# Tile 1's attention weights ahead of the turning of the edge records and of tile 0's counts, in a graph network on one core

## The reference

```python
# block 0: attention over the incoming edges of each node
a = hs @ Ws.T + h[dst] @ Wd.T + emb_rel[etype] @ Wr.T      # hs = h[src]
e = leaky_relu((a @ attn_fc2_w.T)[:, 0], 0.01)
w = exp(e - segment_max(e, dst)[dst])
alpha = w / segment_sum(w, dst)[dst]
agg = segment_sum(alpha[:, None] * hs, dst)                # h itself where a node has no edge
x = layernorm(x + agg + h @ loop_weight)
# block 1: two layers of the same form
agg = segment_sum((rel_embed[rel_id] + h[src]) @ W_r, dst)
h = rrelu(agg * deg ** -0.5 + (h @ W_el if no edge else h @ W_sl))
x = layernorm(x + h)
```

## Time and profile before

| | us |
|---|---|
| median of 3 runs | 2778.87 (2776.01 to 2779.62) |
| the profiled execution | 2776.1 |
| its span | 2774.0 |
| tile loop, about | 105 to 2167 |
| PE busy | 2149.1 (77%) |
| DVE busy | 2045.1 (74%) |
| POOL busy | 1591.4 (57%) |
| ACT busy | 1223.8 (44%) |

### The profile page before, as it was taken

How to read it: one execution, slowest core, us unless ns; L and a number is a source line. 1 busy time by engine, 2 the same in 40 slices (tenths; PEclk the granted TensorE clock), 3 DMA queues, 4 the chain that set the end, 5 groups by cost and what they waited for, 6 DMA issues and landing times.

```text
span 2774.0 us, 45483 instructions
## 1 busy us (share of the span) xinstructions
PE 2149.1 (77%) x16208; PEld 1802.6 (65%) x16208; DVE 2045.1 (74%) x4582; ACT 1223.8 (44%) x3215; POOL 1591.4 (57%) x1672
## 2 busy tenths in 40 slices
PE   1366676667767777777787788788787999999998
PEld 0255565556666666666676676676675876888887
DVE  5889998887888888888888888888797456333333
ACT  1255665555556456555555555555555323000000
POOL 6767777777777777777777777777774000000000
PEclk9988887888888988888889888999899999999999
DMA  8545554554555554554555555555454354666664
GB/s 219 145 126 173 173 153 153 157 165 152 160 175 151 156 181 146 159 183 148 160 186 151 160 190 153 168 183 156 148 177 152 112 156 133 215 211 211 217 211 158
DMA packets 184632, 463.50 MB, mean 167 GB/s; under 512 B 86336, under 2 KB 113784, under 8 KB 164577
## 3 DMA queue, kind: packets, MB, share of 16 engines
q1 hardware_dynamic: 116050, 339.10, 36.4%
q0 software_dynamic: 53600, 114.17, 16.4%
q10 hardware_dynamic: 14752, 7.26, 1.0%
HBM read 362.54 MB, written 97.84 MB: 166 GB/s over the span
## 4 chain that ended last, share of the span: by engine, by line
POOL 50%; PE 25%; issue 17%; DVE 6%; DMA 1%; ACT 1%; SPq 1%; ACTq 0%; POOLq 0%; DVEq 0%
POOL arena L559 50%; PE pair L951 19%; DVE arena L1114 2%; PE bank L875 1%; PE pair L924 1%; PE bank L836 1%; PE pair L954 1%; DMA wlp<-n_L_gnn_loop_weight_dram 1%; DVE arena L1084 1%; PE pair L805 1%; PE pair L782 0%; DMA group_starts<-endv 0%; SPq L434 0%; DVE arena L1194 0%; DVE arena L1092 0%
## 5 line engine op out<-in xcount | busy, mean ns | idle before, releaser
L559 POOL DMA_INDIRECT arena<-rows,srcw x1617 | 1541.6, 953 | 518.8 <-issue 491.4
L1114 DVE TENSOR_TENSOR arena<-bank,idx 128x2000 bf16<-128x2000 bf16 (+3 forms) x700 | 560.4, 853 | 21.1 <-PE pair L805 17.9
L951 PE MATMUL pair<-arena 125*125 125x384 bf16 x3285 | 551.4, 326 | 1.6 <-DVE arena L1316 1.6
L805 PE MATMUL pair<-arena 128*128 128x250 bf16 x2500 | 348.9, 287 | 260.0 <-DVE arena L1114 206.5
L581 ACT ACTIVATE arena<-pair 99x264 f32<-99x264 f32 (+2 forms) x410 | 279.0, 712 | 593.8 <-PE pair L805 448.5
L951 PEld LDWEIGHTS pair<-arena 125*125 125x125 bf16 x3285 | 447.4, 136 | 103.3 <-issue 8.4
L675 ACT ACTIVATE arena<-arena,wexp 128x128 f32<-128x128 bf16 x1650 | 487.4, 387 | 1.6
L875 PE MATMUL bank<-arena 128*125 128x130 f32 x3300 | 485.2, 318 | 0.0
L875 PEld LDWEIGHTS bank<-arena 128*125 128x125 f32 x3300 | 474.6, 230 | 4.2
L805 PEld LDWEIGHTS pair<-arena 128*128 128x128 bf16 x2500 | 239.7, 102 | 339.4 <-DVE arena L1114 267.0
L1084 DVE TENSOR_TENSOR arena<-arena,bank 128x4224 bf16<-128x4224 int16 x150 | 344.2, 2350 | 1.7
(11 more groups left out here) (250 smaller groups left out, 2312.6 us busy)
## 6 DMA issues: line engine op xcount, KB each, us to landing
arena<-counts SPq DMA_DIRECT2D x106, 812.5 KB, 4.4
counts<-arena SPq DMA_DIRECT2D x50, 1562.5 KB
arena<-dst SPq DMA_DIRECT2D x50, 1056.0 KB
arena<-etype SPq DMA_DIRECT2D x50, 1056.0 KB
arena<-rows,srcw POOLq DMA_INDIRECT x1617
arena<-counts SPq DMA_DIRECT2D x14, 281.2 KB, 2.8
edge_terms<-arena SPq DMA_DIRECT2D x200, 12.4 KB
xt<-in_x_dram SPq DMA_DIRECT2D x50, 62.5 KB
```

Source lines behind the costliest of these rows:

```text
L559: pool.indirect_dma_start(out=rows[:, q, c, :], out_offset=None, in_=rows0, in_offset=bass.IndirectOffsetOnAxis(ap=srcw[:, q, c:c + 1], ax ...
L805: r = pe.matmul(group_of(n, gi), ohl[:, sl, gi * GC + c, :], ohm[:, sl, gi * GC + c, :], start=(c == 0), stop=(c == GC - 1))
L951: r = pe.matmul(o, ring[0:TN, m % RD, h - h0, :], hs[k][0:TN, h, :], start=(h == first), stop=(h == last - 1))
L1114: return v.tensor_tensor(hot_.rearrange("p c (j t) -> p c j t", t=2), iotap[:, 0:w].rearrange("p (j t) -> p j t", t=2)[:, None, :, :].broa ...
```

## The change

The copies, turns and evacuations of the edge records and the seven count batches of tile 0 leave the first turn and stand in the second: on DVE after `weights(1)` and `prepare_wide(2)`, on PE and ACT after `terms(2)`. `normalise(0)`, `x1_in(0)`, `x1_node(0)`, `node_t(0)` and `node_a(0, 0)`, which stood behind them, so follow at once. PE's `row(0)` comes after the batches of tile 0. `SEQ` is renumbered to fit. POOL's and SP's code is not touched.

```diff
@@ SEQ
     if t_ == 0:
         SEQ["types", 1] = len(SEQ)
         SEQ["turned", 1] = len(SEQ)
+        continue
+    if t_ == 1:
         for b_ in range(NGB):
             SEQ["idx", b_] = len(SEQ)
+        for j_ in range(BT):
+            SEQ["cnt", 0, j_] = len(SEQ)
@@ ACT
                     types_in(1)
                     types(1)
-                    for b in range(NGB):
-                        n = seq("idx", b)
-                        act_evac(act, n, idx[...], slot(n)[...])
-                    for j in range(BT):
-                        batch(0, j)
                     node_t(0)
                     node_a(0, 0)
                 elif t < NT - 1:
+                    if t == 1:
+                        for b in range(NGB):
+                            n = seq("idx", b)
+                            act_evac(act, n, idx[...], slot(n)[...])
+                        for j in range(BT):
+                            batch(0, j)
@@ PE
-                if 1 <= t < NT - 1:
-                    row(t - 1)
-                if t == 0:
-                    types_in(1)
-                    types(1)
+                if t == 1:
                     for b in range(NGB):
...
                     for j in range(BT):
                         batch(0, j)
+                if 1 <= t < NT - 1:
+                    row(t - 1)
+                if t == 0:
+                    types_in(1)
+                    types(1)
                     x1_in(0)
                     x1_node(0)
@@ DVE
                 if t == 0:
                     finalize(0)
                     prepare_edges(1)
+                    normalise(0)
+                if t == 1:
                     for b in range(NGB):
...
                     for j in range(BT):
                         batch(0, j)
-                    normalise(0)
-                elif more:
+                if t >= 1 and more:
                     for j in range(2):
                         batch(t, j)
```

More of the change, by code:

```diff
@@ L686, in act_fast @@
                     types(1)
-                    for b in range(NGB):
-                        n = seq("idx", b)
-                        act_evac(act, n, idx[:, b * GB:(b + 1) * GB, :], slot(n)[:, :].rearrange("p (m g) -> p g m", g=GB))
-                    for j in range(BT):
-                        batch(0, j)
                     node_t(0)
@@ L694, in act_fast @@
                 elif t < NT - 1:
+                    if t == 1:
+                        for b in range(NGB):
+                            n = seq("idx", b)
+                            act_evac(act, n, idx[:, b * GB:(b + 1) * GB, :], slot(n)[:, :].rearrange("p (m g) -> p g m", g=GB))
+                        for j in range(BT):
+                            batch(0, j)
                     for j in range(3):
@@ L1302, in dve_fast @@
                         batch(t, j)
-                else:
+                if not more:
                     finalize(t)
```

## The result

| | before | after |
|---|---|---|
| median (7 runs each) | 2777.42 us (2776.01 to 2779.62) | 2785.93 us (2785.13 to 2790.54) |
| ratio, 95% interval | | 1.0032 (1.0023 to 1.0041) |
| the profiled execution | 2776.1 us | 2787.2 us |
| its span | 2774.0 us | 2785.0 us |

The kernel became 8.5 us slower, by the medians. The forecast was 2787.6, with a range of 2781 to 2793, and 8.7 us for the change itself. Of the 1.7 us between the forecast and the measured 2785.9, 1.5 are the starting value: the forecast stood on a median before of 2778.87 from three runs, and seven runs give 2777.42.

The account below looks back on a forecast made before the run. POOL's gather chain was taken to bound the kernel; tile 3's gather, starting at 192.4 instead of 183.65, adds 8.7 us to the 2778.9 median, with nothing else moving the end: 2787.6 us, range 2781 to 2793.

Parts of the forecast that it names:

- DVE's gap near 140, for tile 1's terms: DVE after normalise(0): idles some 6 us from 140.1, as the load of tile 1's terms is no longer covered by records.
- `node_in(0, 0)`: Tile 0's node step on DVE: begins 2.5 us after PE's x1_in(0) at 145.0, so at 147.5 instead of 168.14.
- tile 1's sums end: PE's weighted sums of tile 1: shifted 20.6 us earlier with weights(1), through at 162.3 instead of 182.9.
- PE's first turn: PE's first turn of the moved records: waits for tile 2's third term evacuation, 164.3 against 144.85, a shift of 19.5 us.
- last count evacuated, then the store: ACT's last evacuation of tile 0's counts: 185.9 instead of 166.4, and SP's store_counts(0) waits for it.
- tile 3's gather begins: POOL: tile 3's lists land 6.1 to 6.9 us after the store, so 192.4 instead of 183.65, 8.7 us later.
- `AT` stored: Store of tile 0's counts: done near 190.5; ACT's first evacuation of tile 1's counts waits, DVE doesn't feel it until 194.6.
- The step that decided the sign: SP's queue: load_lists(3) stands behind store_counts(0), so late counts delay tile 3's lists and POOL's gather by 8.7 us.
- Slow landing: Rival: tile 3's type list lands 7.6 us after issue behind the store; POOL starts at 197.5, 13.9 us late, 2792.7; chance 0.10.
- The second rival: Tile 3's lists arrive before POOL is free; it stops one tile later, tile 4's gather at 224.3; 2778.3 us; chance 0.08.
- The full gain of 10.5 us: Rival: lists don't gate and DVE is early too, tile 2's sums through by 214.4; POOL keeps 10.5 us, 2768.4; chance 0.03.
- The floor of 2.1 us for a small DMA to land: Loads of tile 1's terms and tile 3's lists: a small DMA lands no sooner than 2.1 us after its issue.

Follow-up runs that it names:

- e1c: The changed kernel, but SP issues tile 3's lists before it waits for tile 0's counts: 2777.07 us, ratio 1.0002 to the kernel before.
- e3c: The kernel before, with SP holding tile 3's lists until ACT has evacuated tile 2's last destination terms: 2783.34 us, ratio 1.0018.
- e9: e5c with tile 1's last four count batches moved behind weights(2) and tile 4's lists ahead of tile 1's counts store: 2774.51 us, ratio 0.9991 to before.
- e5c: The changed kernel with tile 3's lists ahead of the counts store and the records turned in the first turn again: 2773.93 us, ratio 0.9987 to before.
- e7: e5c, but with prepare_edges(2) between tile 0's second and third batch: 2777.08 us, ratio 0.9998 to the kernel before.
- e1b_lists_first: The changed kernel with load_lists(3) ahead of store_counts(0), on a second chip where the kernel before took 4547 us: 4550.30 us, ratio 1.0007.
- p1: The kernel before, with POOL waiting after every eighth gather until all gathers so far have landed: 3407.87 us, ratio 1.2255.

## Why the prediction was right

By its own steps, forecast against the trace after:

| step | forecast | measured |
|---|---|---|
| DVE's gap near 140, for tile 1's terms | 6 us | 5.98 |
| `node_in(0, 0)` | 147.5 | 147.13 |
| `z` of tile 1 done | 151.2 | 150.7 |
| tile 1's sums end | 162.3 | 162.5 |
| PE's first turn | 164.3 | 164.67 |
| last count evacuated, then the store | 185.9 | 185.77, 185.79 |
| tile 3's gather begins | 192.4 | 192.17 |
| stall ahead of it | 19.6 us | 19.78 |
| tile 0's batches on DVE end | 183.9 | 183.81 |
| `AT` stored | 190.5 | 191.2 |
| tile 2's sums end | 224.0 | 224.46 |
| `u` of tile 3 | 245.1 | 245.65 |
| last gather | 2132 | 2132.04 |
| DVE waits for rows | more than 41 tiles | 42, 160.4 us |

DVE's timeline after carries most of these:

```profile
138.90 0.35 DVE L1193 TENSOR_SCALAR arena<-arena,mv,nv 125x128 f32<-125x128 f32 x1
145.22 0.20 DVE L1142 TENSOR_TENSOR dr<-drw 128x33 f32<-128x33 f32 x1 [5.98 <-DMA drw<-edge_terms]
...
147.13 0.35 DVE L1200 SCALAR_TENSOR_TENSOR arena<-bank,iso,slt 125x128 f32<-125x128 f32 x1 [0.63 <-ACT slt L645]
...
150.52 0.20 DVE L1171 TENSOR_TENSOR z<-le,M 128x33 f32<-128x33 f32 x1
...
183.81 0.41 DVE L1233 COPY idx<-arena 128x100 bf16<-128x100 bf16 x2
```

*The releasers.* The change did what it says: DVE reached tile 1's weights some 20 us sooner, and PE's sums were through at 162.5, ten before POOL was free. The step that decided the sign was the second thing that POOL needs. SP's wait at its store changed its releaser from tile 1's scaling to the last count evacuation. SP's waits show it (who waited for what, us in total, times, longest); the longest is the one ahead of this store. In the kernel after:

```profile
SPq L474 <- ACT arena L621: 59.4, 3, 33.7
```

Three such waits, 59.4 us in all, stand against two of 22.2 us in the kernel before. Moving this one item in SP's list took the 8.5 us away (`e1c`), and making it late by itself cost 4.5 us on POOL (`e3c`). Both directions of the step are shown. What neither run separates is whether the store, once issued, slows the lists behind it: the lists' report came 2.3 us after the type list's issue in the kernel after and 2.0 in `e3c`.

The Trainium skill ("DMA: Bandwidth & Descriptors", Rules for kernel authors) says to issue a DMA early and wait for it late. The runs agree, with a ratio of 1.0032 for the late lists against 1.0002 for the early ones. The statement of the Trainium skill on queues (same page, Queues, rings and completion order), that a semaphore's increment follows the earlier writes of the same DMA engine, is compatible with what is seen: the store was done at 191.2 and the lists were reported at 192.17. No run here shows that the one had to wait for the other.

*The rivals.* Slow landing didn't come: the type list landed 2.3 us after its issue. The second rival, no change because the lists don't gate, was built as `e1c`. Its working gave tile 4's gather at 224.3 and a gain of 0.6 us; measured were 224.66 and no difference that can be told from the kernel before. The full gain of 10.5 us was not reached by `e9` either: POOL still waits 4.34 us for tile 2's sums, for which the prediction gave the reason, DVE's late weights of tile 2, and 3.58 us more for tile 3's.

*The sizes.* The profiled execution grew by 11.0 us in its span, 8.5 up to the last gather and 2.5 behind it. The 2.5 go with TensorE's clock, and not with a wait that the change makes. From the end of the last tile's weighted sums to the end of the span lie 613.8 us in both kernels. What differs is the stretch from the last gather to the end of those sums, 36.6 us before and 39.2 after. Most of that is one group of products on PE, `row(48)`, which took 8.15 us before and 9.83 us after:

```profile
2127.18 8.15 PE L836 MATMUL bank<-arena 125*125 125x384 bf16 x49 [2.06 <-DVE arena L1203]
2136.22 9.83 PE L841 MATMUL bank<-arena 125*125 125x384 bf16 x49 [2.03 <-DVE arena L1209]
```

Over this group the clock granted to TensorE was 1.00 of full speed before and 0.83 after (the number behind the five busy times, of PE, its weight loads, DVE, ACT and POOL; the DMA share and GB/s follow):

```profile
2127.00:2135.50 8.50, 8.32 (x52) 6.98 (x52) 3.87 (x7) 0.00 (x0) 0.00 (x0) 1.00 0.98 370
2136.00:2146.00 10.00, 9.78 (x50) 7.82 (x51) 3.90 (x7) 0.00 (x0) 0.00 (x0) 0.83 0.98 374
```

PE had been idle equally long ahead of the group, 2.06 and 2.03 us. In the kernel after the clock was then mostly at the lower of its two levels, 0.50 (1.2 GHz), from 2137 to 2141 (means of 0.59 and 0.55 over the two halves). It was at 0.50 from 2131 to 2133 as well, where two products ahead of `row(48)` took 1.40 us in place of 0.91; that is most of the 0.5 us by which the group begins later behind the last gather.

The profiles of `e1c`, `e3c` (the kernel before but for its late lists), `e5c`, `e7` and `e9` have 0.83 to 0.85 there and 9.53 to 9.83 us for the group, and 651.8 to 653.5 us from the last gather to the end, against 650.5 before and 653.0 after. So the profiled execution of before was a short one, as the prediction said of its place among the runs. Why the clock stayed at full speed in it isn't shown. The medians, which differ by 8.5 us, are the better measure of the change.

*What was weaker in it.* That tile 1's sums ended within 0.2 us of the forecast is in part luck. DVE was through with `z` 0.5 us sooner than forecast, and PE's sums took 10.16 us in place of 9.52, at a granted clock of 0.74 against 0.79 before; the sum had no term for the clock there. The floor of 2.1 us for a small DMA to land was read from the source lists; the destination terms were reported 1.94 us after their issue (143.28 to 145.22). The landing of `AT` was given as 190.5 and came at 191.2, harmless here. In `e7` I treated that same landing as free, and the whole expected gain was lost to it.

## What to carry to other kernels

Before moving work ahead, write down for each waiting engine all the things that it waits for, and ask for each of them what is queued in front of it: here the stall's named releaser was taken 20 us forward, while the second condition went back by more than 12 us, because its DMA stood in SP's list behind a store that went from 173.14 to 185.79. Before, the lists were there by 180.0 at the latest and POOL began at 183.65, so some 4 us of the 12 were spare, and 8.5 were lost. Loads on which the bounding engine depends belong ahead of a queue's waits for slow results. And where one engine does 25 us of one-time work, moving it by a turn moves the stall by a tile; of the orders tried, those that split it between turns, as in `e5c`, gave something back, and less than the stall's size: in `e5c` POOL still waits 6.03 us for tile 2's sums, and the attempt to shorten that path further (`e7`) took away the cover of the single buffer `AT`.

## What the runs showed of the hardware

- On two chips the same program took 4501 and 4547 us in place of 2777. The profiles of the five experiments there show ACT waiting for up to 42.8 us and DVE for up to 39.0, with "remote" as releaser, and POOL waiting for PE's sums in 47 or 48 tiles. DVE's timeline of `e1b_lists_first` shows one such place. POOL had issued its last gather before it at 3049.32:

```profile
3056.24 1.80 DVE L1122 TENSOR_TENSOR arena<-bank,idx 128x2000 bf16<-128x2000 bf16 x2 [38.00 <-remote]
```

  The ACT instruction that waits 42.20 us beside it, at 3056.25, is an evacuation of 128 x 1000 elements, the form that in `e7_edges_early` waits for the store of `AT`; its line, L587, is a helper's and stands for all evacuations. A store that isn't reported before the gathers around it are through would look like this. That is argued only. The cause stays open, since `p1` ran where it didn't occur.
- The store of `AT`, 1.6 MB, was reported to ACT 5.4 us after its issue in the kernel after (185.79 to 191.2) with POOL idle, and 7.2 us in `e7_edges_early` with POOL gathering (187.79 to 195.03). In `e1c_lists_first` it was 7.3 us (185.21 to 192.49). POOL's gathers aren't the only difference: in `e1c` and `e7` SP issues the two broadcast loads of 1 MB each 1.0 us after the store, in the kernel after 5.1 us after it. No run separates the two. With one buffer, that is time in which the next tile's counts stand.
- The issue of a small list load cost SP 0.37 us in one place and 1.18 us in another (`dstw` of tile 3 in `e3c`, and right behind the store in the kernel after). That made up 0.8 of the 1.1 us by which the lists were slower there. The store isn't the only thing that brings the longer issue: in `e5c_records_stay` `dstw` took 1.33 us at 153.16 and in `e7_edges_early` `etw` 1.22 us at 154.67, with no store ahead of them for 9 us.
